# Moving seven of eight expert-output gathers and additions out of the expert layer and into the first tile of the cross attention

## The chip, the core and the metric

The kernel runs on one core of a Trainium2 chip. The metric is device time in microseconds (us) for one execution. A core has five engines that run their own instruction streams and meet through semaphores: PE (TensorE, matrix products, with its weight loads shown as PEld), DVE (VectorE), ACT (ScalarE), POOL (GpSimd) and SP (SyncE, which here issues the plain DMAs). POOL issues the indirect DMAs, which gather rows of memory by an index.

## The reference, cut to what matters

The model takes x, 16 x 64 tokens of width 512, and a context of 16 x 512 rows of width 384, and applies six layers, each as x = x + layer(layernorm(x)):

```
x = x + cosine similarity of x with the context
x = x + self attention (16 heads)
x = x + experts: 8 experts, each token goes to its best 2
x = x + cross attention to the context (16 heads of 64)
x = x + decayed attention, a scan
x = x + feed forward with rounding
```

The layer that the change starts in, in the reference:

```
scores = softmax(xf @ w_gate);  weights, idx = top_k(scores, 2)
...each expert computes its tokens' rows: exp_out...
gathered = exp_out[flat_e, pos_c]
w = weights.reshape(-1)[:, None] * vmask
out = (gathered * w).reshape(N, TOP_K, d).sum(axis=1)
```

So the last step of the expert layer is, for each token, to fetch two rows of 512 numbers and to add them to x, each times its weight. The layer behind it, the cross attention, begins with the layernorm of the new x:

```
q = x @ Wq;  k = context @ Wk;  v = context @ Wv
out = softmax(q k^T * scale) v @ Wo + bo
```

## The kernel before, in words

x stays in SBUF as [128 partitions, 8 token tiles (+1 spare), 512]; a token tile is 128 tokens. Everything is float32.

**Expert layer** (`expert_layer`, L636). A first block routes: the two best experts of each token, their weights (`top`), and the row (`slot`) that each copy of a token takes in a table in memory. A second block runs 23 steps; each loads 128 rows of the table and an expert's weights, multiplies (L901, L885) and stores 128 rows of results in `yg_d`, called routed_y in the profile. Behind the steps comes the part that the change touches. POOL (L971 to L980) waits for all stores, and then issues for each of the 8 token tiles two indirect gathers, one for each chosen expert, into `yb`, a buffer with room for 4 tiles. It is the old `xn`, called xnall in the profile. DVE (L960 to L968) waits for a tile's two gathers and does two `scalar_tensor_tensor` operations on it, x = gathered * weight + x (L963), the second after the first has ended. Nothing else runs on the core then.

Between layers the program clears the semaphores of the last layer on all engines (`reset_sems`, L2002) and opens those of the next (`open_sems`, L1992). All engines meet there, so the cross attention starts when DVE's last addition is done.

**Cross attention** (`cross_attention_layer`, L983). A start part computes for token tile 0 the layernorm (DVE statistics L131 to L134, one power on POOL L139, DVE L145, PE transposes L152), and the queries (L1120) and the queries through Wk (L1134). Then `tile(i)` runs for the 8 token tiles: seven in a loop, the last written out behind it. A tile has 16 pairs of heads g = 0 to 15 (PAIRS). For each pair, in a software pipeline over the engines:

- PE `scores` of pair g + 2 (split product of 9 matmuls, L106), then `turn` of pair g (4 transposes of the normalized exponentials, L1098), and at g = 5, 9 and 13 a `weigh` (36 matmuls, L106).
- ACT: `exponent` (L1203), then copies that take the high part of operands (L1207 to L1220).
- DVE, in this order in each g: the reciprocal (L1324), the normalization of `pb` (L1325, which `turn` waits for), `rest_q` for pair g + 3 (L1299, qs, which `scores` of that pair waits for), `rest_P` of pair g - 1 (L1299, pT), `maximum` of pair g + 2 (L1294), and in some g the low parts of the context, `rest_T` at g = 3 to 5 and `rest_N` at g = 0 to 3, 11 and 12 (L1299, cT and cN). At g = 6 and 7 come the next tile's layernorm statistics and L145.

Behind the 16 pairs PE does the next tile's queries, the last `weigh`, the head outputs (L1165), which ACT copies to the buffer `oT`, and the output product with `oT` (L1176), whose bias row `bo` (L1177) comes from W0. DVE adds the result to x (L1347). `oT` is thus written and read only near the end of a tile. POOL's only work in the layer is L139, once a tile.

The order on each engine is as written in the program; the position of an operation in DVE's stream is where the code of `tile` puts it.

Of the kernel before, what the change touches and what calls it, by code (L numbers as in the profile page):

```python
# [15 lines left out]
P = 128  # L16
# [54 lines left out]
BASE = 1  # L71
# [564 lines left out]
def expert_layer(nc, a, e):  # L636
# [13 lines left out]
    with ExitStack() as st:  # L650
# [3 lines left out]
        xn = sbuf("xnall3", [P, NT, D])  # L654
        slot = sbuf("slot3", [P, NT, 2], U32)
        top = sbuf("top3", [P, NT, 2])
        owner = sbuf("owner3", [1, ET], I32)
# [9 lines left out]
        y_mm, y_sb = sem("y_mm3"), sem("y_sb3")  # L667
        s_yb = [sem(f"s_yb3_{n}", pool_dma=True) for n in range(NT // 2)]
        added, half = sem("added3"), sem("half3")

# [154 lines left out]
        y = sbuf("y3", [P, 2, D])  # L825
        YB = NT // 2
        yb = xn
        TURNS = (ET - 3) // 2
# [11 lines left out]
        with nc.Block() as block:  # L840
# [97 lines left out]
            @block.vector  # L938
            def _(ve):
                def y_take(s, u, pair):  # L940
                    ve.wait_ge(y_mm, BASE + s + 1)
                    ve.wait_ge(y_out[u], BASE + 16 * pair)
                    nc.vector.tensor_copy(y[:, u, :], ps[7]).then_inc(y_sb, 1)

                def step(s, u, pair):
                    if not (isinstance(s, int) and s < 2):
                        y_take(s - 2, u, pair - 1)
                    ve.wait_ge(silu_sb, BASE + s + 1)
                    ve.wait_ge(gl_mm, BASE + s + 1)
                    ve.wait_ge(hT_mm, BASE + 2 * s)  # L950
                    for c in range(2):
                        ins = nc.vector.tensor_tensor(hid[:, c * HFE:(c + 1) * HFE], gated[:, c * HFE:(c + 1) * HFE],  # L952
                                                      ps[2 + c][:, 0:HFE], ALU.mult)
                    ins.then_inc(hid_sb, 1)

                steps(ve, step)
                y_take(ET - 2, 1, (ET - 2) // 2)
                y_take(ET - 1, 0, (ET - 1) // 2)

                for t in range(NT):  # L960
                    ve.wait_ge(s_yb[t % YB], 32 * (t // YB + 1))
                    for c in range(2):
                        ins = nc.vector.scalar_tensor_tensor(x[:, t, :], yb[:, t % YB * 2 + c, :], top[:, t, c:c + 1],  # L963
                                                             x[:, t, :], ALU.mult, ALU.add)
                        if c == 0:
                            ins.then_inc(half, 1)
                            ve.wait_ge(half, BASE + t + 1)
                    ins.then_inc(added, 1)  # L968

            @block.gpsimd  # L970
            def _(pool):  # L971
                for u in range(2):
                    pool.wait_ge(y_out[u], BASE + 16 * ((ET + 1 - u) // 2))
                for t in range(NT):
                    if t >= YB:
                        pool.wait_ge(added, BASE + t - YB + 1)
                    for c in range(2):
                        nc.gpsimd.indirect_dma_start(
                            out=yb[:, t % YB * 2 + c, :], out_offset=None, in_=yg_d,
                            in_offset=bass.IndirectOffsetOnAxis(slot[:, t, c:c + 1], axis=0)).then_inc(s_yb[t % YB], 16)  # L980


def cross_attention_layer(nc, a, e):  # L983
# [23 lines left out]
    with ExitStack() as st:  # L1007
# [14 lines left out]
        xT = W0[:, 15360:15872].rearrange("p (k t) -> p k t", k=DK)  # L1022
        bo = W0[0:1, 15872:16384]
        nmax, rsum, rinv = sbuf("nmax4", [P, 4]), sbuf("rsum4", [P, 4]), sbuf("rinv4", [P, 4])
# [6 lines left out]
        ct_hi, ct_lo, cn_hi, cn_lo = sem("ct_hi4"), sem("ct_lo4"), sem("cn_hi4"), sem("cn_lo4")  # L1031
        y_mm, added = sem("y_mm4"), sem("added4")
        work = [ps[4], ps[5], ps[7]]

# [8 lines left out]
        with nc.Block() as block:  # L1043
# [22 lines left out]
            @block.gpsimd  # L1066
            def _(pool):
                ln.pool(pool, 0)
                with pool.Fori(0, NT - 1) as i:
                    ln.pool(pool, i + 1)  # L1070

# [119 lines left out]
            def _(act):  # L1191
# [55 lines left out]
                def tile(i, last):  # L1247
# [19 lines left out]
                    if not last:  # L1267
                        queries(use + U_Q, U_Q)
                        for c in range(CK):
                            first_T(i + 1, 0, c)  # L1270
                    weighed(i, 3)
                    for n in range(2):
                        take(use + U_O + n, U_O + n, oT[:, 4 * n:4 * n + 4, :].rearrange("p m t -> p (m t)"))
# [15 lines left out]
            def _(ve):  # L1289
# [27 lines left out]

                def tile(i, last):
                    maximum(i, 0)
                    maximum(i, 1)  # L1320
                    for g in range(PAIRS):
# [12 lines left out]
                        for u, j in SPLIT_N.get(g, []):  # L1334
                            rest_N(i, u, j)
                        if g == 6 and not last:
                            ln.vector_stats(ch, i + 1)
# [16 lines left out]
                for g in range(QB):  # L1354
                    rest_q(0, g)
                with ve.Fori(0, NT - 1) as i:
                    ch.turn(i, 2 + PAIRS)
                    tile(i, False)
                ch.again(NT - 1)
                tile(NT - 1, True)  # L1360

# [583 lines left out]
def perceiver_kernel(nc, a, out):  # L1945

    ctx = ExitStack()
    with ctx:
# [67 lines left out]

        env = Env()
        env.x, env.cn, env.W0, env.PS, env.ps, env.ident, env.ones = x, cn, W0, PS, ps, ident, ones
        env.out, env.xg_d, env.yg_d, env.v_d, env.ba_d = out, xg_d, yg_d, v_d, ba_d
# [68 lines left out]
```

## Time and profile before

| | |
|---|---|
| time, median of 3 runs | 2352.98 us (2350.37 to 2353.34) |
| profiled execution: its own time | 2354.67 us |
| profiled execution: span of the trace | 2352.8 us |
| PE busy | 2090.8 us (89%) |
| DVE busy | 1084.6 us (46%) |
| ACT busy | 930.5 us (40%) |
| POOL busy | 123.4 us (5%) |

The span is cut into stretches by the layers: the expert layer's steps end at about 811 us, its gathers and additions at 839 us, and the cross attention runs from 844 to 1709 us in eight tiles of about 107 us. Busy shares are averages over all of it: in the 36 us from 810 to 846 us PE is busy for 0.48 us, in most of a cross attention tile for all of the time.

A row of a timeline reads: start in us, duration in us, engine, line, operation, output<-input, shape, count merged into this row, and in brackets how long the engine had been idle and what it waited for. PEld rows are PE's weight loads. "[... <-issue]" is a gap for which the profile shows no wait. Each of DVE's operations on 512 columns lasts longer than the step to the next one, since the next starts while it ends.

### The profile page before, as it was taken

The numbers are of one execution on the slowest core, as the hardware profiler recorded it, in microseconds if no ns is written. First come the engines' busy times: TensorE is split into PE (matmuls) and PEld (weight loads), VectorE is DVE, ScalarE is ACT, GpSimd is POOL, SyncE is SP. The second block draws the span as 40 slices with busy tenths as digits, with TensorE's granted clock in tenths as the row PEclk, the third lists the DMA queues.
The fourth block names the chain that finished last, engine by engine and source line by source line (L and its number), as shares of the span: only waits on it lengthen the run. The fifth ranks groups of instructions, "written<-read, shape, count | busy, mean of one in ns | idle before, by whom it ended". The sixth has DMA issues, their size and how long they took to land. (4 is left out here: it accounts for less than half of the span.)

```text
span 2352.8 us, 30151 instructions
## 1 busy us (share of the span) xinstructions
PE 2090.8 (89%) x9904; PEld 1469.2 (62%) x9904; DVE 1084.6 (46%) x2172; ACT 930.5 (40%) x1699; POOL 123.4 (5%) x138
## 2 busy tenths in 40 slices
PE   7979962999999759999999999999979499877999
PEld 5647862555555348787878777787757377633443
DVE  4655552010100135444352626343355599839992
ACT  5743320111111034445454545444344477615550
POOL 0000013000000110000000000000000000002220
PEclk9989875999999979999999999999989555588999
DMA  7410024777778421010000001010021700000000
GB/s 258 132 38 1 0 103 174 306 290 311 310 289 319 173 85 41 15 52 27 27 27 27 27 27 40 13 40 27 1 90 45 252 1 1 1 5 0 1 14 23
DMA packets 35591, 212.41 MB, mean 90 GB/s; under 512 B 5059, under 2 KB 5060, under 8 KB 27974
## 3 DMA queue, kind: packets, MB, share of 16 engines
q1 hardware_dynamic: 32966, 203.28, 22.9%
q0 software_dynamic: 2560, 8.39, 1.1%
q8 instruction: 25, 0.41, 0.1%
q14 instruction: 40, 0.33, 0.0%
HBM read 189.04 MB, written 22.61 MB: 90 GB/s over the span
## 5 line engine op out<-in xcount | busy, mean ns | idle before, releaser
L106 PE MATMUL PS<-cT,qs 128*128 128x512 f32 x1152 | 293.5, 400 | 7.0 <-ACT pb L1203 7.0
L106 PE MATMUL PS<-pT,cN 128*128 128x512 f32 x1152 | 270.3, 392 | 1.7 <-DVE pT L1299 1.7
L106 PEld LDWEIGHTS PS<-cT,qs 128*128 128x128 f32 x1152 | 208.4, 188 | 57.1 <-issue 15.1
L901 PE MATMUL PS<-W,xgT 128*128 128x384 f32 x736 | 242.8, 488 | 1.4 <-ACT xgT L924 1.4
L106 PEld LDWEIGHTS PS<-pT,cN 128*128 128x128 f32 x1152 | 213.9, 188 | 45.5 <-DVE pT L1299 1.9
L901 PEld LDWEIGHTS PS<-W,xgT 128*128 128x128 f32 x736 | 140.4, 191 | 104.2 <-issue 11.3
L1198 ACT ACTIVATE qp<-PS 128x512 f32<-128x512 f32 x192 | 110.9, 596 | 196.8 <-PE PS L106 189.8
L106 PE MATMUL PS<-ws,xT 128*128 128x512 f32 x672 | 170.2, 412 | 11.4 <-DVE ws L1510 6.3
L1294 DVE TENSOR_REDUCE nmax<-PS 128x1 f32<-128x512 f32 x128 | 87.7, 685 | 160.5 <-PE PS L106 160.4
L106 PEld LDWEIGHTS PS<-ws,xT 128*128 128x128 f32 x672 | 131.9, 200 | 46.8 <-issue 18.0
L952 DVE TENSOR_TENSOR hid<-gated,PS 128x384 f32<-128x384 f32 x46 | 23.4, 551 | 277.5 <-PE PS L877 235.6
L1705 PEld LDWEIGHTS PS<-cn,W1s 128*128 128x128 f32 x512 | 114.0, 328 | 49.5 <-DVE W1s L1633 45.3
L885 PE MATMUL PS<-W,hT 128*128 128x512 f32 x276 | 124.5, 600 | 10.4 <-ACT hT L918 10.4
L1705 PE MATMUL PS<-cn,W1s 128*128 128x16 f32 x512 | 120.8, 376 | 11.8 <-DVE W1s L1633 11.8
L1804 PE MATMUL PS<-xT,W 128*128 128x512 f32 x256 | 121.0, 624 | 6.4 <-ACT h L1847 5.6
L152 PE MATMUL PS<-cn,xn 128*128 128x128 f32 x200 | 40.7, 339 | 95.7 <-DVE xn L145 83.5
L1299 DVE TENSOR_TENSOR qs<-qp,qs 128x384 fp32r<-128x384 f32 x128 | 69.3, 552 | 115.4 <-ACT qs L1207 115.4
L1814 PE MATMUL PS<-W,hs 128*128 128x512 f32 x256 | 112.7, 592 | 0.5 <-DVE hs L1910 0.5
L1299 DVE TENSOR_TENSOR pT<-PS,pT 128x512 fp32r<-128x512 f32 x128 | 87.0, 685 | 56.1 <-ACT pT L1220 56.1
L931 ACT ACTIVATE gated<-PS 128x384 f32<-128x384 f32 x46 | 20.0, 488 | 227.2 <-PE PS L901 227.2
L139 POOL TENSOR_TENSOR rs<-ve,cn 128x1 f32<-128x1 f32 x51 | 28.0, 549 | 1561.9 <-DVE ve L134 1561.9
L1203 ACT ACTIVATE pb<-PS,nmax 128x512 f32<-128x512 f32 x128 | 87.5, 684 | 34.3 <-DVE nmax L1294 34.2
(225 smaller groups left out, 3161.1 us busy)
## 6 DMA issues: line engine op xcount, KB each, us to landing
W<-in_fc SPq DMA_DIRECT2D x23, 3072.0 KB, 12.6
W<-in_proj SPq DMA_DIRECT2D x23, 1536.0 KB, 6.7
cT<-in_ctxT SPq DMA_DIRECT2D x16, 768.0 KB, 5.7
ct_in<-in_ctxT SPq DMA_DIRECT2D x16, 768.0 KB, 4.3
cn_in<-in_ctxN SPq DMA_DIRECT2D x16, 768.0 KB, 5.0
W<-in_w SPq DMA_DIRECT2D x2, 4096.0 KB, 24.5
routed_x<-zero SPq DMA_DIRECT2D x23, 256.0 KB, 5.4
xg<-routed_x SPq DMA_DIRECT2D x23, 256.0 KB, 5.8
```

Of the source, the lines that this page charges most:

```text
L106: mm = nc.tensor.matmul(out, lhs(m, s), rhs(n, s), start=(opens and (s, m, n) == terms[0]), stop=((s, m, n) == terms[-1]))
L139: self.nc.gpsimd.tensor_tensor(self.rs[:, :], self.ve[:, :], self.cn[:, CN_MHALF:CN_MHALF + 1], ALU.pow).then_inc(self.rstd, 1)
L152: last = self.nc.tensor.transpose(self.bank[:, k * P:(k + 1) * P], self.xn[:, k * P:(k + 1) * P], self.ident)
L885: mm = nc.tensor.matmul(ps[7], hT[:, f, :], pj[u][:, f, :], start=(f == 0), stop=(f == FK - 1))
L901: mm = nc.tensor.matmul(ps[c][:, 0:HFE], xgT[:, k, :], fc[u][:, k, c * HFE:(c + 1) * HFE], start=(k == 0), stop=(k == DK - 1))
L1198: nc.scalar.activation(out, src, ACT.Copy, scale=scale).then_inc(w_sb, count)
L1203: nc.scalar.activation(pb[:, g % 2, :], ps[g % 2], ACT.Exp, bias=nmax[:, g % 4:g % 4 + 1], accum_out=rsum[:, g % 4:g % 4 + 1]).then_inc(e_ ...
L1294: nc.vector.tensor_reduce(nmax[:, g % 4:g % 4 + 1], ps[g % 2], AX.X, ALU.max, negate=True).then_inc(m_dve, 1)
L1299: return nc.vector.tensor_tensor(out, whole, first.bitcast(F32), ALU.subtract)
L1705: mm = nc.tensor.matmul(ps[u][:, col:col + B], rb[:, j % RB, k * P:(k + 1) * P], sel, start=True, stop=True)
L1804: mm = nc.tensor.matmul(ps[n % HB], w16[:, k, f * P:(f + 1) * P], xT[g][:, k, :], start=(k == 0), stop=(k == DK - 1))
L1814: mm = nc.tensor.matmul(ps[HB + t % ZB], hs[:, t // TG, f, (t % TG) * P:(t % TG + 1) * P], w26[:, f, :], start=(f == 0), stop=(f == FT - 1))
```

## The change

All but the first token tile's gathers and additions leave the expert layer. The expert layer gathers tile 0's two rows and adds them. In the cross attention POOL gathers tiles 1 to 7 one after the other into `oT` (seen as `got`, room for one tile), each gather waiting until the additions of the tile before have read the buffer (`routed`). DVE does tile t's two additions at the end of its work for pair g in tile 0: tile 1 at g = 1, then 2 at 3, 3 at 5, 4 at 8, 5 at 10, 6 at 12 and 7 at 14. POOL issues gathers 1 to 4, then does the power for tile 1's layernorm, then issues gathers 5 to 7. ACT waits for all additions ahead of its copies into `oT`.

So that this fits, `slot` and `top` move into a free place of W0, `bo` moves from W0 to the spare row of x, and DVE's tile 0 is written out ahead of its loop, which now runs over tiles 1 to 6. The loops of PE and ACT stay.

```diff
@@ expert_layer @@
-        slot = sbuf("slot3", [P, NT, 2], U32)
-        top = sbuf("top3", [P, NT, 2])
+        slot, top = e.slot, e.top
...
-                for t in range(NT):
-                    ve.wait_ge(s_yb[t % YB], 32 * (t // YB + 1))
-                    for c in range(2):
-                        ins = nc.vector.scalar_tensor_tensor(x[:, t, :], yb[:, t % YB * 2 + c, :], top[:, t, c:c + 1],
-                                                             x[:, t, :], ALU.mult, ALU.add)
-                        if c == 0:
-                            ins.then_inc(half, 1)
-                            ve.wait_ge(half, BASE + t + 1)
-                    ins.then_inc(added, 1)
+                ve.wait_ge(s_yb, 32)
+                for c in range(2):
+                    nc.vector.scalar_tensor_tensor(x[:, 0, :], xn[:, c, :], top[:, 0, c:c + 1], x[:, 0, :],
+                                                   ALU.mult, ALU.add).then_inc(half, 1)
+                    ve.wait_ge(half, BASE + c + 1)
...
-                for t in range(NT):
-                    if t >= YB:
-                        pool.wait_ge(added, BASE + t - YB + 1)
-                    for c in range(2):
-                        nc.gpsimd.indirect_dma_start(
-                            out=yb[:, t % YB * 2 + c, :], out_offset=None, in_=yg_d,
-                            in_offset=bass.IndirectOffsetOnAxis(slot[:, t, c:c + 1], axis=0)).then_inc(s_yb[t % YB], 16)
+                for c in range(2):
+                    nc.gpsimd.indirect_dma_start(
+                        out=xn[:, c, :], out_offset=None, in_=yg_d,
+                        in_offset=bass.IndirectOffsetOnAxis(slot[:, 0, c:c + 1], axis=0)).then_inc(s_yb, 16)
+                pool.wait_ge(s_yb, 32)
@@ cross_attention_layer @@
-        bo = W0[0:1, 15872:16384]
+        bo = x[0:1, NT, :]
...
+        got = oT[:, :, :].rearrange("p (c k) t -> p c (k t)", c=2)
+        ROUTED_AT = {1: 1, 3: 2, 5: 3, 8: 4, 10: 5, 12: 6, 14: 7}
@@ gpsimd @@
+                def gather(t):
+                    if t > 1:
+                        pool.wait_ge(routed, BASE + 2 * (t - 1))
+                    for c in range(2):
+                        nc.gpsimd.indirect_dma_start(
+                            out=got[:, c, :], out_offset=None, in_=e.yg_d,
+                            in_offset=bass.IndirectOffsetOnAxis(e.slot[:, t, c:c + 1], axis=0)).then_inc(s_got, 16)
                 ln.pool(pool, 0)
-                with pool.Fori(0, NT - 1) as i:
-                    ln.pool(pool, i + 1)
+                for t in range(1, 5):
+                    gather(t)
+                ln.pool(pool, 1)
+                for t in range(5, NT):
+                    gather(t)
+                pool.wait_ge(s_got, 32 * (NT - 1))
+                with pool.Fori(0, NT - 2) as i:
+                    ln.pool(pool, i + 2)
@@ scalar @@
+                    act.wait_ge(routed, BASE + 2 * (NT - 1))
                     for n in range(2):
                         take(use + U_O + n, U_O + n, oT[:, 4 * n:4 * n + 4, :].rearrange("p m t -> p (m t)"))
@@ vector @@
+                def add_routed(t):
+                    ve.wait_ge(s_got, 32 * t)
+                    for c in range(2):
+                        nc.vector.scalar_tensor_tensor(x[:, t, :], got[:, c, :], e.top[:, t, c:c + 1], x[:, t, :],
+                                                       ALU.mult, ALU.add).then_inc(routed, 1)
+                        ve.wait_ge(routed, BASE + 2 * (t - 1) + c + 1)
...
                         for u, j in SPLIT_N.get(g, []):
                             rest_N(i, u, j)
+                        if first and g in ROUTED_AT:
+                            add_routed(ROUTED_AT[g])
...
-                with ve.Fori(0, NT - 1) as i:
-                    ch.turn(i, 2 + PAIRS)
-                    tile(i, False)
+                ch.turn(0, 2 + PAIRS)
+                tile(0, True, False)
+                with ve.Fori(0, NT - 2) as i:
+                    ch.again(i + 1)
+                    tile(i + 1, False, False)
                 ch.again(NT - 1)
-                tile(NT - 1, True)
+                tile(NT - 1, False, True)
@@ perceiver_kernel @@
+        env.slot = W0[:, 15872:15888].bitcast(U32).rearrange("p (t c) -> p t c", t=NT)
+        env.top = W0[:, 15888:15904].rearrange("p (t c) -> p t c", t=NT)
```

## Rows read from the trace of the kernel before

**Rows 1.** The timeline of the expert layer's end, all engines.

```profile
818.35 1.54 DVE L963 SCALAR_TENSOR_TENSOR x<-xnall,top,x 128x512 f32<-128x512 f32 x2 [7.14 <-DMA xnall<-routed_y,slot]
818.55 1.37 POOL L978 DMA_INDIRECT xnall<-routed_y,slot  x1 [0.30 <-issue]
...
837.92 1.54 DVE L963 SCALAR_TENSOR_TENSOR x<-xnall,top,x 128x512 f32<-128x512 f32 x2 [1.40 <-DMA xnall<-routed_y,slot]
```

**Rows 2.** The gathers of L978 by their line: duration min/median/max, and landing.

```profile
L978 POOL DMA_INDIRECT xnall<-routed_y,slot x16: 942/952/1379, 813.5 to 834.2; - x16
...
DMA to landing us min/median/max: 3.4/3.7/3.9
```

**Rows 3.** The additions of L963 by their line: duration of one, min/median/max in ns.

```profile
L963 DVE SCALAR_TENSOR_TENSOR x<-xnall,top,x x16: 751/752/753, 818.3 to 838.7; 128x512 f32<-128x512 f32 x16
```

**Rows 4.** The timeline of the cross attention's start.

```profile
843.69 0.69 DVE L131 BATCH_NORM_STATS2 st<-x 128x6 f32<-128x512 f32 x1 [4.23 <-PEq L1994]
...
844.99 0.57 POOL L139 TENSOR_TENSOR rs<-ve,cn 128x1 f32<-128x1 f32 x1 [9.89 <-DVE ve L134]
...
846.20 1.12 PE L152 MATMUL PS<-cn,xn 128*128 128x128 f32 x4 [35.72 <-DVE xn L145]
```

**Rows 5.** Stretches: length, busy us (instructions) of each engine, PE clock, DMA share, GB/s.

```profile
409.00:410.00 1.00, 0.90 (x4) 0.71 (x4) 0.00 (x0) 0.00 (x0) 0.00 (x0) 0.50 0.88 356
413.00:414.00 1.00, 1.00 (x3) 0.63 (x2) 0.00 (x0) 0.00 (x0) 0.00 (x0) 0.57 1.32 555
...
814.00:816.00 2.00, 0.00 (x0) 0.00 (x0) 0.00 (x0) 0.00 (x0) 1.44 (x2) 0.50 0.35 82
...
854.00:855.00 1.00, 1.00 (x10) 1.00 (x10) 0.00 (x0) 0.10 (x1) 0.00 (x0) 0.91 0.00 0
...
938.00:955.00 17.00, 17.00 (x137) 15.28 (x137) 2.63 (x5) 4.55 (x8) 0.00 (x0) 1.00 0.15 47
```

**Rows 6.** The timeline of tile 0, pairs g = 2 to 7.

```profile
879.71 0.16 DVE L1324 RECIPROCAL rinv<-rsum 128x1 f32<-128x1 f32 x1
...
885.77 0.15 DVE L1324 RECIPROCAL rinv<-rsum 128x1 f32<-128x1 f32 x1
...
889.36 0.42 PEld L1098 LDWEIGHTS PS<-cn,pb 128*128 128x128 f32 x4 [0.48 <-DVE pb L1325]
...
889.78 8.44 PE L106 MATMUL PS<-pT,cN 128*128 128x512 f32 x36
...
891.49 0.16 DVE L1324 RECIPROCAL rinv<-rsum 128x1 f32<-128x1 f32 x1
...
900.29 0.69 DVE L1294 TENSOR_REDUCE nmax<-PS 128x1 f32<-128x512 f32 x1 [7.05 <-PE PS L106]
```

**Rows 7.** The timeline of tile 0, pairs g = 9 to 15.

```profile
907.18 0.49 DVE L1325 TENSOR_SCALAR pb<-pb,rinv 128x512 f32<-128x512 f32 x1
...
907.88 0.59 PEld L1098 LDWEIGHTS PS<-cn,pb 128*128 128x128 f32 x4
...
920.22 0.49 DVE L1325 TENSOR_SCALAR pb<-pb,rinv 128x512 f32<-128x512 f32 x1
...
920.62 0.55 DVE L1299 TENSOR_TENSOR qs<-qp,qs 128x384 fp32r<-128x384 f32 x1
...
921.95 0.69 DVE L1294 TENSOR_REDUCE nmax<-PS 128x1 f32<-128x512 f32 x1 [0.17 <-PE PS L106]
922.08 1.93 PEld L106 LDWEIGHTS PS<-cT,qs 128*128 128x128 f32 x9
...
926.68 0.16 DVE L1324 RECIPROCAL rinv<-rsum 128x1 f32<-128x1 f32 x1
...
927.42 0.42 PEld L1098 LDWEIGHTS PS<-cn,pb 128*128 128x128 f32 x4 [0.81 <-DVE pb L1325]
...
930.50 0.16 DVE L1324 RECIPROCAL rinv<-rsum 128x1 f32<-128x1 f32 x1
...
935.90 1.03 PEld L1098 LDWEIGHTS PS<-cn,pb 128*128 128x128 f32 x8
```

More of the change, by code:

```diff
@@ L667, in expert_layer @@
         y_mm, y_sb = sem("y_mm3"), sem("y_sb3")
-        s_yb = [sem(f"s_yb3_{n}", pool_dma=True) for n in range(NT // 2)]
-        added, half = sem("added3"), sem("half3")
+        s_yb = sem("s_yb3", pool_dma=True)
+        half = sem("half3")
         def load_fc(sp, u, own):
@@ L825, in expert_layer @@
         y = sbuf("y3", [P, 2, D])
-        YB = NT // 2
-        yb = xn
         TURNS = (ET - 3) // 2
@@ L1032, in cross_attention_layer @@
         y_mm, added = sem("y_mm4"), sem("added4")
+        s_got, routed = sem("s_got4", pool_dma=True), sem("routed4")
+        got = oT[:, :, :].rearrange("p (c k) t -> p c (k t)", c=2)
+        ROUTED_AT = {1: 1, 3: 2, 5: 3, 8: 4, 10: 5, 12: 6, 14: 7}
         work = [ps[4], ps[5], ps[7]]
@@ L1316, in rest_P, with tile @@
                          turned(pT[0], g)).then_inc(pt_sb, 1)
-                def tile(i, last):
+                def add_routed(t):
[4 more added lines that the diff above has]
+                        ve.wait_ge(routed, BASE + 2 * (t - 1) + c + 1)
+                def tile(i, first, last):
                     maximum(i, 0)
```

## The prediction, made before the changed kernel was run

> **What bounds the kernel now.** I read the timeline across the layer boundary first, then the two operations of the moved part by their lines, then tile 0 of the cross attention pair by pair, asking at each place for an addition who waits for DVE there.
>
> At the expert layer's end nothing runs but the gathers and the additions. DVE begins tile 0's two additions at 818.35 and tile 7's at 837.92, each pair 1.54 us long, and idles for gathers between them [rows 1]. The next layer's first statistics start at 843.69, 4.23 us after the last addition, and DVE waited there for the meeting of the engines [rows 4]. So the seven tiles' share of the tail stands on the path whole.
>
> Tile 0 of the cross attention has two kinds of stretches. Between the `weigh` blocks DVE works without a gap from g = 1 to g = 5 and PE waits for it: the reader is to see the 0.48 us in front of `turn(5)` at 889.36, put down to DVE's `pb`, and the 0.81 us before `turn(13)` at 927.42 [rows 6, 7]. During a `weigh`, 36 matmuls in 8.44 us from 889.78 on, it is DVE that idles: 7.05 us until 900.29 [rows 6]. An addition in the first kind costs its length; in the second it is free. Behind the last pairs PE is busy without a gap (17.00 of 17.00 us from 938 to 955, [rows 5]), and DVE's next tile start hangs on PE, so a shift that PE has by `weigh(2)` is carried to the end and is not given back.
>
> **What it removes.** The meeting of the engines follows tile 0's additions instead of tile 7's: 837.92 - 818.35 = 19.57 us off the path [rows 1]. The 4.23 us between the layers stay [rows 4]; a few semaphores fewer to clear I count as nothing. Tile 0's own gathers come as before, so nothing new is late there.
>
> **What the additions cost in tile 0.** One lasts 752 ns with hardly any spread [rows 3]; two with the wait between them take 1.54 us [rows 1], and the wait behind the second, which before had only the layer's end behind it, adds another 0.04. So 1.58 us per token tile, in order of the stream:
>
> - Tiles 1 and 2, at g = 1 and 3: in the stretch where DVE has no gap. Everything behind them to `pb` of pair 5 shifts, and `turn(5)`, which already waited, shifts with it. 2 x 1.58 = 3.16 us.
> - Tile 3, at g = 5: behind `pb` of pair 5. PE is in `weigh(0)`; DVE has 7.05 us [rows 6]. 0.
> - Tile 4, at g = 8: before `pb` of pair 9, ready at 907.18 + 0.49 = 907.67 where `turn(9)` loads at 907.88 [rows 7]: slack 0.2. 1.4 us.
> - Tile 5, at g = 10. The code puts it behind `maximum` of pair 12, whose scores come only behind `weigh(1)`; so it isn't hidden by that block, but stands before the normalization at 920.22. `rest_q` at 920.62 feeds the scores at 922.08, and the `maximum` at 921.95 had waited only 0.17 [rows 7]. 1.58 - 0.17 = 1.4 us.
> - Tile 6, at g = 12, before the reciprocal at 926.68; `turn(13)` waits for DVE already [rows 7]. 1.58 us.
> - Tile 7, at g = 14, before the reciprocal at 930.50, while PE is in `weigh(2)` until 935.90 [rows 7]. The normalization of pair 15 would end at 931.2, so there is room for 4.7 us. 0.
>
> Sum 3.16 + 1.4 + 1.4 + 1.58 = 7.54 us.
>
> **Whether the gathers come in time.** One buffer now serves all, so gather t + 1 is asked for when additions t have ended. From there to data: 0.1 for POOL to see it (my choice, from the power that starts right behind the statistics, [rows 4]), 0.95 for the first issue, 0.30 to the next [rows 1, 2], 3.7 from the second's issue to its landing [rows 2]. 5.05 us. DVE's own work between two additions is the time it has: 885.77 - 879.71 = 6.06 us for tile 2; 891.49 - 885.77 = 5.72 for tile 3, and 5.5 more of idle [rows 6]; over 13 for tiles 4 and 5; 926.68 - 920.22 + 0.2 = 6.66 for tile 6; 930.50 - 926.68 = 3.82 for tile 7, which waits 1.2 and with its additions uses 2.8 of the 4.7 that are free [rows 7]. All fit, tile 2 by 1.0 us. Tile 1's is asked for at the layer's start and is early by far. Behind POOL's waits stands only the power for tile 1's layernorm, behind gather 4, which is issued some 5 us before DVE's statistics at g = 6; 0. No plain DMA is queued behind the gathers, as SP issues those. They share the DMA engines with the context loads, which could hold gather 7 up; it has 1.9 us left.
>
> Two prices no row shows. POOL now issues gathers while DVE is busy with other operations than the additions. A gather that met additions took 1.37 instead of 0.95 us and ended with them, at 819.92, while no addition was slowed (751 to 753 ns) [rows 1 to 3]. By that only the gathers lengthen, by 0.4 each at most or 5.9 us in all, still under 6.06. At worst normalizations behind additions 1, 2, 4 and 5 wait out an issue of 0.95, or both: up to 7.6 us. At best 0. I take 0.8, near the rows, which show the additions untouched.
> The Trainium skill, in "SBUF — State Buffer", section "Who interferes with whom", says that DVE in a two-port mode and GpSimd exclude each other for a whole instruction, whoever came first. The row above agrees on the side of the gather; for DVE's side no row here has a normalization beside a gather. By that rule the upper end would be the case, and it is the first rival below.
>
> The PE clock: PE is at 0.50, that is 1.2 GHz, by 814, and will be so when the layer begins in either kernel. It is at full clock 7.9 us after PE's first work at 846.20 here, but 4.8 us after that at 409.1 at the expert layer's start [rows 4, 5]. So it may come up to 3.1 us sooner, worth half of that: -1.6 to, by symmetry, +1.6. I take -0.5.
>
> The wait on ACT ahead of `oT` is long met when it comes. DVE's written-out tile, the moved `bo`, `slot` and `top` do the same operations: 0, with nothing beside them that could hide a price.
>
> **The sum.** -19.57 + 7.54 + 0.8 - 0.5 = -11.7 us. The profiled execution, 2354.67 us around a span of 2352.8, would become 2343.0. It lies 1.69 above the median of the runs shown, 2352.98, from which I forecast 2341.3 us.
>
> **The rivals.**
> - DVE and POOL exclude each other. For it: the lengthened gather. Against it: the untouched additions. Price: four normalizations wait 0.95 or twice that, 3.8 to 7.6 in place of 0.8: 2344.3 to 2348.1.
> - The additions find more room than I see: part of the shift is made up when PE comes out of a `weigh` with DVE's work done, and the clock rises early. For it: `turn` waits under a microsecond for DVE. Against: the waits are of the right engine, and nothing idles on PE that could absorb. 2 us less on the additions and 1.1 on the clock: 2338.2.
> - The gathers become the bound. If DVE starves POOL until one request takes G instead of 5.05 us, additions 2, 3, 6 and 7 wait G - 6.06, G - 11.2, G - 6.66 and G - 6.95 (3.82 and the 3.1 of room left). It decides from G = 10.5 on, where the first, third and fourth sum to 11.8, the whole gain. At G = 12: 5.9 + 0.8 + 5.3 + 5.1 = 17.1, so 2358.4. Against it: the longest of 16 issues was 1.38 us, with two-input additions beside it.
> - It does not do what it says, and the end of the layer was held by something beside the seven tiles (the meeting itself, or POOL's waits): no difference, 2353. Against: DVE's rows wait for gathers one by one.
>
> **How the numbers follow.** Forecast 0.60 (its own range 2339.5 to 2343.7, from the ends of clock and waits), exclusion 0.23, more room 0.09, gathers the bound 0.04, no difference 0.04. What this measurement can tell from no change is 0.2%, 4.7 us, so 2348.3 and below is faster: 0.60 + 0.23 + 0.09 less a little of the exclusion's upper end gives 0.91; same 0.05; slower 0.04. The range leaves out the last two and the very end of the first: 2337.5 to 2347.5.
>
> **What would show it.** The statistics that start the cross attention at about 824.1 instead of 843.69. Seven `scalar_tensor_tensor` pairs of 1.54 us in tile 0. `weigh(0)` 3.2 us later behind the layer's start than before, `weigh(1)` 4.6, `weigh(2)` 7.5. DVE waiting for a gather only before tile 7's, about 1.2 us. Wrong if DVE waits for gathers at g = 3 or 12, if normalizations (L1325) last over their 0.49 us, if POOL's issues last 2 us or more, or if tile 1 is shifted otherwise than `weigh(2)`.

## The result, and the profile after

The changed kernel takes 2341.13 us (median of 5 runs, 2338.00 to 2342.99) against 2352.98 us before (5 runs, 2348.99 to 2353.34). The medians differ by 11.9 us. The ratio, taken between the means, is 0.9954, 95% interval 0.9942 to 0.9967: 0.46% or 10.8 us faster. Predicted were 2341.3 us, 2337.5 to 2347.5. Run again beside the first experiments it took 2342.34 us against 2352.68, ratio 0.9954 (0.9940 to 0.9968).

The profiled execution of the changed kernel took 2338.00 us around a span of 2336.1, 16.7 us less than that of before, more than the medians differ by. Cut at landmarks, the two spans say why:

| stretch | before | after | difference |
|---|---|---|---|
| start to the expert layer's first gather | 813.50 | 809.97 | -3.53 |
| first gather to the cross attention's first statistics | 30.19 | 10.56 | -19.63 |
| those to the addition of tile 0's output into x | 131.59 | 140.31 | +8.72 |
| that to the addition of tile 7's output | 732.52 | 732.56 | +0.04 |
| that to the end | 645.0 | 642.7 | -2.3 |

The first and the last row lie in code that the change leaves alone; they are spread between executions. In the repeat the first gather comes at 811.32 and the last stretch is 644.7. The change itself is -19.63 + 8.72 = -10.9 us.

The tail of the expert layer after the change, in the timeline (start us, us, engine, line; in brackets the idle time before), answers to [rows 1] and [rows 4]:

```profile
809.97 0.98 POOL L968 DMA_INDIRECT xnall<-routed_y,W  x1 [411.64 <-SPq L837]
811.25 0.96 POOL L968 DMA_INDIRECT xnall<-routed_y,W  x1 [0.30 <-issue]
814.63 1.54 DVE L959 SCALAR_TENSOR_TENSOR x<-xnall,W,x 128x512 f32<-128x512 f32 x2 [6.95 <-DMA xnall<-routed_y,W]
820.53 0.69 DVE L131 BATCH_NORM_STATS2 st<-x 128x6 f32<-128x512 f32 x1 [4.35 <-PEq L2017]
```

One pair of additions where eight stood, and the same 4.35 us between the layers (4.23 before).

DVE's stream in tile 0 with the additions in it, from the same timeline:

```profile
856.41 1.53 DVE L1332 SCALAR_TENSOR_TENSOR x<-oT,W,x 128x512 f32<-128x512 f32 x2
857.98 0.16 DVE L1342 RECIPROCAL rinv<-rsum 128x1 f32<-128x1 f32 x1
...
864.05 1.53 DVE L1332 SCALAR_TENSOR_TENSOR x<-oT,W,x 128x512 f32<-128x512 f32 x2
...
871.36 1.53 DVE L1332 SCALAR_TENSOR_TENSOR x<-oT,W,x 128x512 f32<-128x512 f32 x2
...
880.18 0.69 DVE L1304 TENSOR_REDUCE nmax<-PS 128x1 f32<-128x512 f32 x1 [5.49 <-PE PS L106]
...
912.73 0.69 DVE L1343 TENSOR_SCALAR pb<-pb,rinv 128x512 f32<-128x512 f32 x1
...
915.72 1.54 DVE L1332 SCALAR_TENSOR_TENSOR x<-oT,W,x 128x512 f32<-128x512 f32 x2 [1.07 <-DMA oT<-routed_y,W]
917.30 0.16 DVE L1342 RECIPROCAL rinv<-rsum 128x1 f32<-128x1 f32 x1
```

From the start of an addition pair to the next reciprocal is 1.57 us. The pair at 871.36 is paid from idle time, which is 5.49 us now and was 7.05 [rows 6]; only tile 7's waits for its gather, 1.07 us. What PE sees, in its timeline (weight loads of the transposes, and the `weigh` blocks):

```profile
866.37 0.42 PEld L1107 LDWEIGHTS PS<-cn,pb 128*128 128x128 f32 x4 [2.53 <-DVE pb L1343]
...
869.64 8.45 PE L106 MATMUL PS<-pT,cN 128*128 128x512 f32 x36
...
890.04 8.46 PE L106 MATMUL PS<-pT,cN 128*128 128x512 f32 x36
...
911.48 0.42 PEld L1107 LDWEIGHTS PS<-cn,pb 128*128 128x128 f32 x4 [2.41 <-DVE pb L1343]
...
911.89 10.06 PE L106 MATMUL PS<-pT,cN 128*128 128x512 f32 x36
```

The last line is the one thing that nobody had in the sum: the same 36 matmuls take 10.06 us, not 8.46. The stretches show the cause (columns as in [rows 5], the clock third from the end):

```profile
905.00:908.00 3.00, 2.62 (x14) 1.87 (x13) 2.96 (x8) 1.89 (x5) 0.19 (x1) 1.00 0.52 156
912.00:913.00 1.00, 1.00 (x6) 0.81 (x5) 0.96 (x4) 0.34 (x1) 0.78 (x1) 0.79 0.99 336
913.00:914.00 1.00, 1.00 (x3) 0.73 (x3) 0.47 (x2) 0.92 (x3) 0.17 (x1) 0.50 0.63 205
915.00:916.00 1.00, 1.00 (x4) 0.81 (x3) 0.28 (x1) 0.00 (x0) 0.00 (x0) 0.51 0.10 37
916.00:917.00 1.00, 1.00 (x5) 0.80 (x5) 0.96 (x2) 0.49 (x1) 0.00 (x0) 1.00 0.00 0
```

PE's clock fell from 2.4 to 1.2 GHz at 912.6, just after PE had waited for DVE before turn(11), (12) and (13), and came back at 916. Its weight loads had idled 0.87, 0.81 and 2.41 us there; in the kernel before they idle only before turn(13), 0.81 us [rows 7].

### The profile page after: what moved, and what is told of

The parts are those of the page before. It is cut to its first block and busy times, and to the rows that moved or that the text cites. A ratio compares the mean times of both kernels' runs of the same rounds, so it can differ in the third digit from the quotient of the medians.

```text
span 2336.1 us, 30096 instructions
## 1 busy us (share of the span) xinstructions
PE 2090.7 (89%) x9904; PEld 1465.4 (63%) x9904; DVE 1084.3 (46%) x2172; ACT 930.7 (40%) x1699; POOL 121.7 (5%) x138
## 5 line engine op out<-in xcount | busy, mean ns | idle before, releaser
L106 PEld LDWEIGHTS PS<-ws,xT 128*128 128x128 f32 x672 | 131.8, 199 | 46.3 <-issue 17.8
```

Of the source, the lines that this page charges most:

```text
L106: mm = nc.tensor.matmul(out, lhs(m, s), rhs(n, s), start=(opens and (s, m, n) == terms[0]), stop=((s, m, n) == terms[-1]))
```

## The experiments

In all of them "tile 0" is the time from the cross attention's first statistics to the addition of tile 0's output, and "the rest" that from the addition of tile 7's output to the end. A `weigh` is given by its start behind the first statistics. Collected from their traces (us; the clock's rise is where PE came to full clock in the start part, to half a microsecond):

| run | tile 0 | weigh(0), (1), (2) | clock's rise | clock's dips in tile 0 | rest |
|---|---|---|---|---|---|
| before | 131.59 | 46.09, 65.20, 84.14 | 10.5 | none | 645.0 |
| changed | 140.31 | 49.11, 69.51, 91.36 | 10.0 | at 92 to 95.5 | 642.7 |
| repeat | 140.03 | 48.89, 69.27, 91.10 | 9.5 | at 91.5 to 95 | 644.7 |
| idle places | 130.23 | 44.67, 63.99, 82.91 | 7.5 | none | 645.1 |
| tile 6 later | 137.10 | 49.12, 69.53, 89.76 | 7.5 | at 45 to 48.5 | 645.2 |
| none | 130.95 | 45.58, 64.73, 83.67 | 9.5 | none | 634.1 |
| one gather | 138.68 | 49.16, 69.53, 91.34 | 7.5 | at 45 to 49 | 644.1 |
| late gathers | 144.69 | 51.96, 72.35, 96.23 | 10.0 | at 47.5 to 51 and at 95 to 98.5 | 643.8 |
| rearranged only | 130.69 | 45.28, 64.44, 83.35 | 9.0 | none | 644.4 |
| idle places, 43 more | 131.75 | 46.21, 65.53, 84.47 | 10.5 | none | 646.6 |
| idle places, 230 more | 130.51 | 44.99, 64.28, 83.17 | 7.5 | none | 636.0 |
| idle places, 212 more | 131.16 | 45.65, 64.96, 83.88 | 9.5 | none | 636.1 |
| before, 72 more | 131.62 | 46.10, 65.26, 84.20 | 10.5 | none | 637.9 |

**Does the dip repeat?** The changed kernel, unchanged.

> The changed kernel again, unchanged, to see what repeats. Measured from the cross attention's first statistics (L131) to the addition of tile 0's output into x, tile 0 took 131.6 us before and 140.3 after: 7.2 us of shift by turn(13), as predicted, and 1.6 us more in weigh(2) (10.06 us instead of 8.46), in which the PE clock was at half from 912.8 to 916. My theory: the additions leave PE waiting before turn(11) to turn(13), and the clock falls for it; then the dip comes again, in weigh(2) or near it, and tile 0 takes 139 to 141 us. Rival: a chance dip that has nothing to do with the change; then it is absent here and tile 0 takes 138.7 us. Time 2341 us; the 3.5 us that the profiled execution was ahead of the one before when the expert layer ended are chance by both and may be gone.

2342.34 us. The dip is there again, in the same block, which takes 10.04 us. It is no chance event of one execution. The expert layer's first gather is at 811.32 instead of 809.97.

**The additions where DVE idles.**

```diff
-        ROUTED_AT = {1: 1, 3: 2, 5: 3, 8: 4, 10: 5, 12: 6, 14: 7}
+        ROUTED_AT = {}
+        EARLY_AT = {6: 4, 10: 5, 14: 6}
...
+                        if first and g in EARLY_AT:
+                            add_routed(EARLY_AT[g])
                         if g + 2 < PAIRS:
                             maximum(i, g + 2)
...
                     rest_P(i, PAIRS - 1)
+                    if first:
+                        add_routed(7)
...
                 ln.vector_norm(ve, 0)
+                add_routed(1)
+                add_routed(2)
                 for c in range(CK):
                     rest_T(0, 0, c)
                 for g in range(QB):
                     rest_q(0, g)
+                add_routed(3)
```

> The same gathers and additions, only at places in DVE's stream where it idles: tiles 1 and 2 between the layernorm and the first rest_T (DVE idle 13.3 us there), tile 3 behind the three rest_q ahead of tile 0, tiles 4 and 5 at g = 6 and 10 ahead of the maximum that waits for a weigh, tile 6 in weigh(2) at g = 14, tile 7 behind the last rest_P. My theory (the additions cost their 1.58 us only where PE waits for DVE, and the clock dip follows from these waits): tile 0 takes 131.6 to 132.4 us instead of 140.3, no dip, time 2341.1 - 8.5 = 2332.6 us. Rival 1 (the gathers themselves, by POOL, the port shared with DVE or DMA traffic, are what costs): tile 0 stays near 138 to 140 us and the time at 2339 to 2341. Rival 2 (gather 2 misses its place, as the room for it is only 0.9 us): 1 to 3 us of the gain are lost, 2334 to 2335.

2333.30 us (2332.53 to 2334.24), ratio to before 0.9917 (0.9904 to 0.9931): 8 to 9 us better than the changed kernel, as expected. Tile 0 takes 130.23 us. Against before all three `weigh` blocks are 1.2 to 1.4 us early. The clock's earlier rise, 3 us at half speed, gives up to 1.6 of that, so at most 0.4 us of seven gathers and fourteen additions is left on the path. The cleaner comparison is between two runs of the table in which the clock rose at the same time: with the additions at idle places (the run with 212 more) tile 0 takes 131.16 us, without any ("none") 130.95. Their price is 0.2 us for all seven. In the timeline, the additions of tile 3 wait 2.88 us for their gather, where PE does not need DVE, and those of tile 4 stand ahead of the `maximum`:

```profile
846.85 1.54 DVE L1333 SCALAR_TENSOR_TENSOR x<-oT,W,x 128x512 f32<-128x512 f32 x2 [2.88 <-DMA oT<-routed_y,W]
...
871.07 1.53 DVE L1333 SCALAR_TENSOR_TENSOR x<-oT,W,x 128x512 f32<-128x512 f32 x2
```

**Only tile 6's additions later.**

```diff
-        ROUTED_AT = {1: 1, 3: 2, 5: 3, 8: 4, 10: 5, 12: 6, 14: 7}
+        ROUTED_AT = {1: 1, 3: 2, 5: 3, 8: 4, 10: 5, 13: 6}
...
                     rest_P(i, PAIRS - 1)
+                    if first:
+                        add_routed(7)
```

> Only the additions of tile 6 move, from g = 12 to g = 13 (into weigh(2)), and those of tile 7 behind the last rest_P of the tile. By the prediction's step for tile 6 turn(13) comes 1.58 us sooner. If the wait of 2.0 us before turn(13) was what let the clock fall, the dip goes too: tile 0 takes 140.3 - 1.6 - 1.6 = 137.1 us, time 2338 us. If the dip is chance, or comes from the waits at turn(11) and turn(12) as well, 138.7 us with it and 137.1 without, in no relation to the edit. If the step is wrong (PE would have waited there anyhow), 140.3.

2339.88 us (2334.29 to 2340.91), tile 0 at 137.10. Tile 0's time is the expected one, but not by the expected parts, and the whole kernel's is 1.9 us above the expected 2338. From weigh(1) to weigh(2) it takes 20.23 us against 21.85 in the changed kernel: 1.62, the step for tile 6. Against the 18.94 of before, 1.29 are left, which is tile 5's. The dip did not go. It moved, to 45 us, in front of weigh(0), where the additions of tiles 1 and 2 make PE wait. There it ate the 1.3 us that an early rise of the clock had given: the additions of tile 1 are 1.29 us earlier than in the changed kernel (34.59 against 35.88), weigh(0) is not (49.12 against 49.11). The stretch of the dip, columns as in [rows 5]:

```profile
869.00:872.50 3.50, 3.50 (x12) 2.78 (x11) 3.46 (x8) 2.20 (x5) 1.12 (x2) 0.53 0.52 149
```

So the wait before turn(13) is one place at which the clock can fall, not the only one.

**Neither gathers nor additions in tile 0.**

```diff
-        ROUTED_AT = {1: 1, 3: 2, 5: 3, 8: 4, 10: 5, 12: 6, 14: 7}
+        ROUTED_AT = {}
...
                 ln.pool(pool, 0)
-                for t in range(1, 5):
-                    gather(t)
                 ln.pool(pool, 1)
-                for t in range(5, NT):
-                    gather(t)
-                pool.wait_ge(s_got, 32 * (NT - 1))
...
-                    act.wait_ge(routed, BASE + 2 * (NT - 1))
```

> Leaves out the gathers and additions of tiles 1 to 7 altogether, so that x lacks the experts' share in these tiles. What is left of the change is the shorter expert tail, the moved buffers and DVE's written-out tile. My theory: tile 0 takes 131.5 us as before, the cross attention starts 10.6 us after the first gather as in the changed kernel, time 2341.1 - 8.8 = 2332.3 us. Rival (the written-out tile costs something, by its code or its first run): tile 0 is 1 us or more above 131.6.

2323.27 us, 9 us less than expected. Tile 0 and the tail are as expected, 130.95 and 10.80. The difference is in the rest, 634.1 us where the runs above had 642.7 to 645.2. The larger part of it, 7.5 us, is in a scan loop of the next layer that the edit does not touch: from DVE's first to its last operation there it takes 180.4 us instead of 187.9 in the two runs of the changed kernel. Nothing of the kind was expected; the last four runs are about it.

**One gather for all additions.**

```diff
-                for t in range(1, 5):
-                    gather(t)
+                gather(1)
                 ln.pool(pool, 1)
-                for t in range(5, NT):
-                    gather(t)
-                pool.wait_ge(s_got, 32 * (NT - 1))
+                pool.wait_ge(s_got, 32)
...
-                    ve.wait_ge(s_got, 32 * t)
+                    ve.wait_ge(s_got, 32)
```

> The additions stay where the changed kernel has them, but only tile 1 is gathered; the additions of tiles 2 to 7 add tile 1's rows again (with their own weights), so x is not the reference's there. It takes away six of the seven gathers from POOL, from the DMA engines and from DVE's waits. My theory: the gathers cost nothing where they stand, so tile 0 takes 140.2 us again, with the dip of the PE clock in weigh(2), time 2341 to 2342 us. Rival (DVE and POOL exclude each other, or the wait of 1.1 us before tile 7's additions reaches PE): tile 0 takes 1 us or more less than in the changed kernel.

2340.55 us against 2341.13 and 2342.34 with all gathers. Tile 0 is 1.4 to 1.6 us shorter, which by the number alone would speak for the rival. The blocks say otherwise: weigh(0) to weigh(1) takes 20.37 us and weigh(1) to weigh(2) 21.81, in the changed kernel 20.40 and 21.85. The difference is weigh(2) itself, 8.46 us, since the dip lay at 45 us here. Six gathers cost under 0.1 us. Whether a dip falls before weigh(0), where PE waits anyhow, or into weigh(2) moves the time by more than that, and goes with where in the start part the clock had risen (7.5 us in both runs with the early dip, 9.5 to 10 in those with the late one). The next run, with longer waits, has a rise at 10 and a dip at either place.

**Gathers 3 us late.**

```diff
                         pool.wait_ge(routed, BASE + 2 * (t - 1))
+                        for k in range(5):
+                            nc.gpsimd.tensor_tensor(W0[:, 15904 + 5 * t + k:15905 + 5 * t + k], cn[:, CN_HALF:CN_HALF + 1],
+                                                    cn[:, CN_MHALF:CN_MHALF + 1], ALU.pow)
```

> POOL does five small powers (0.55 us each) ahead of the gathers of tiles 2 to 7, so that a gather takes G = 8.0 us from its request to its data instead of the 5.0 measured. The prediction's rule for late gathers: additions 2, 3, 6 and 7 wait G - 6.06, G - 11.2, G - 6.66 and G - 6.95 beyond what is hidden, so 1.9 + 0 + 1.3 + 1.1 = 4.3 us: tile 0 takes 140.2 + 4.3 = 144.5 us, and more if the longer waits of PE bring further dips of the clock (1.6 us each), time 2345 to 2348 us. Rival: DVE's waits overlap those it had, or the additions of tiles 4 and 5 are late as well: tile 0 below 142 or above 148.

2345.49 us, ratio to before 0.9973 (0.9963 to 0.9983); tile 0 at 144.69. DVE's waits for gathers, in its timeline:

```profile
868.62 1.54 DVE L1335 SCALAR_TENSOR_TENSOR x<-oT,W,x 128x512 f32<-128x512 f32 x2 [1.66 <-DMA oT<-routed_y,W]
...
878.59 1.54 DVE L1335 SCALAR_TENSOR_TENSOR x<-oT,W,x 128x512 f32<-128x512 f32 x2 [2.00 <-DMA oT<-routed_y,W]
...
916.64 1.54 DVE L1335 SCALAR_TENSOR_TENSOR x<-oT,W,x 128x512 f32<-128x512 f32 x2 [1.58 <-DMA oT<-routed_y,W]
...
926.18 1.54 DVE L1335 SCALAR_TENSOR_TENSOR x<-oT,W,x 128x512 f32<-128x512 f32 x2 [4.03 <-DMA oT<-routed_y,W]
```

From the start of tile 1's additions to tile 2's it is 9.41 us, less 1.57 for the additions: G = 7.8. Tiles 2 and 6 wait 1.66 and 1.58 us, about what the rule said (1.9 and 1.3); tile 3's wait is hidden as it said, since weigh(0) to weigh(1) takes 20.39 us here and 20.40 in the changed kernel; tile 7's was to cost 1.1 and costs nothing, since weigh(2) to the tile's end takes 48.5 us here and 48.9 in the changed kernel. In its place there is a second dip of the clock, one from 47.5 to 51 and one from 95 to 98.5, of which 1.15 us fall into weigh(2) (9.61 us). Tile 0 is as long as expected, but one part of the sum is not what was expected.

**The rearrangement alone.** The kernel before with these edits:

```diff
-        slot = sbuf("slot3", [P, NT, 2], U32)
-        top = sbuf("top3", [P, NT, 2])
+        slot, top = e.slot, e.top
...
-        bo = W0[0:1, 15872:16384]
+        bo = x[0:1, NT, :]
...
-                with ve.Fori(0, NT - 1) as i:
-                    ch.turn(i, 2 + PAIRS)
-                    tile(i, False)
+                ch.turn(0, 2 + PAIRS)
+                tile(0, False)
+                with ve.Fori(0, NT - 2) as i:
+                    ch.again(i + 1)
+                    tile(i + 1, False)
...
+        env.slot = W0[:, 15872:15888].bitcast(U32).rearrange("p (t c) -> p t c", t=NT)
+        env.top = W0[:, 15888:15904].rearrange("p (t c) -> p t c", t=NT)
```

> The kernel before with nothing but the rearrangement of the change: slot and top in W0, bo in the spare row of x, DVE's tile 0 written out ahead of its loop. My theory: no price, tile 0 takes 131.6 us (131.0 to 131.8), time 2352.7 us. Rival: the longer program of DVE moves the later loops in the instruction stream. In the run without additions three stalls of 2.6 us on DVE in the scan of the next layer, which the profile puts down to issue, are gone, though that code is the same; if placement does this, they may be gone here too, and the time some 8 to 10 us less.

2352.41 us, ratio 1.0002 (0.9992 to 1.0011): no price. Tile 0 is 0.9 us shorter by an earlier rise of the clock, and the stalls in the scan are all there, 8.4 us in three.

**Where the scan's stalls come from.** Four runs. The first three start from the kernel with the additions at idle places. The first of them puts 43 increments of an unused semaphore (`pad`) into DVE's stream ahead of the last tile:

```diff
                 ch.again(NT - 1)
+                for _ in range(43):
+                    ve.sem_inc(pad)
                 tile(NT - 1, False, True)
```

> The kernel with the additions at DVE's idle places, and 43 increments of an unused semaphore in DVE's stream ahead of the last cross attention tile, where DVE idles. In the run without gathers and additions the rest of the kernel behind the last cross attention tile took 634.1 us instead of 645, with three issue stalls of 2.6 us fewer in DVE's scan loop. Its DVE program is about 21 instructions shorter; 43 more is the same place by a raster of 64, 32 or 16 instructions. Theory A (the place of the loop in the instruction stream decides): the rest takes 634 to 636 us, time 2323 to 2325. Theory B (the data: x without the experts' share in seven tiles): the stalls stay, 645 us, time 2333.5. If A holds with another raster than these, the stalls stay too, so only the first outcome decides.

2338.85 us: slower than without the 43 by 5.5 us between the medians and 5.2 between the profiled executions. Of the 5.2, 1.5 are in tile 0 by a late rise of the clock, 1.8 between it and tile 7's output, where the 43 stand, and 1.5 in the rest. The scan itself is 4.1 us longer, 192.0 us against 187.9; the part before it happens to be 2.3 us shorter. The stalls did not go; there are more. DVE's waits in the scan, by their sum, times and longest, for this kernel:

```profile
DVE W1s L1650 <- issue: 7.6, 3, 2.6
DVE W1s L1655 <- issue: 3.6, 3, 1.2
```

and for the kernel before:

```profile
DVE W1s L1617 <- issue: 7.8, 3, 2.7
```

The data are the same in this run as in the one without the 43, and so is the scan's code. So the place of the code changes the stalls, though not in the raster that was expected. The next two put 230 and 212 where DVE idles in the last tile:

```diff
                     rest_P(i, PAIRS - 1)
                     if first:
                         add_routed(7)
+                    if last:
+                        for _ in range(230):
+                            ve.sem_inc(pad)
```

> The kernel with the additions at DVE's idle places, and 230 increments of an unused semaphore in DVE's stream, this time in the last cross attention tile behind the last rest_P, where DVE idles for over 20 us. The Trainium skill, in 'Runtime: NRT & Kernel Launch', section 'Instruction fetch mechanics', says that an engine holds two blocks of 256 instructions and that a branch to a block outside them waits for a fetch. By that, the scan's loop stalls at each of its three jumps back unless it starts early enough in a block; the run without additions (some 14 to 22 instructions fewer, no stall, 26 instruction packets on queue q14 instead of 40) would just fit, the others just not, and a move by 256 less these 14 to 22 would bring it to fit again; 230 is meant to overshoot by a few. Theory A (place in the instruction stream): no issue stall in the scan, about 26 packets on q14, the rest behind the last cross attention tile 634 to 636 us instead of 645.1, time 2323 to 2325 us. Theory B (the stalls went for another reason, such as the data of the run without additions): three stalls of 2.6 us or more stay, 645 us or more, time 2333.

> As the run with 230 increments, with 212. By theory A the loop lies 18 instructions earlier in its block: still without stalls if it starts at least so far into a block, otherwise it begins in the block before and stalls return. Either outcome bounds the room; the rest behind the last cross attention tile is 634 to 636 us, or 643 and more.

2325.41 us with 230 (2324.50 to 2326.88), ratio to before 0.9885 (0.9868 to 0.9901), and 2325.33 in the one execution with 212. The rest is 636.0 and 636.1 us, 9 less than without them, and the scan itself 180.3 and 180.2 instead of 187.9. DVE's scan has one wait left, the first. For the kernel with 230, its waits there and its DMA queues:

```profile
DVE W1s L1651 <- ACT W1s L1693: 13.3, 1, 13.3
```

```profile
q8 instruction: 25, 0.41, 0.1%
q14 instruction: 27, 0.22, 0.0%
```

For the kernel before:

```profile
q14 instruction: 40, 0.33, 0.0%
```

The packets that fetch instructions went from 40 to 27 with the stalls. Of the versions that do all of the work this is the fastest: 27 us or 1.15% less than before, and 16 less than the changed kernel in its own runs. The last run puts 72 into the kernel before, at the same place:

```diff
                     rest_P(i, PAIRS - 1)
+                    if last:
+                        for _ in range(72):
+                            ve.sem_inc(pad)
```

> The kernel before, with nothing but 72 increments of an unused semaphore in DVE's stream in the last cross attention tile, behind the last rest_P. DVE's program ahead of the scan is some 100 to 107 instructions shorter there than in the kernel that lost its stalls with 212 and with 230; blocks of 256 then put the loop at the same place with 56 to 81. If the place of the scan's loop in the instruction stream is all there is to it, the three issue stalls go here as well, tile 0 stays at 130.2 to 131.7 us, and the time is 2352.5 - 9 to 10 = 2343 us, without any of the change. Rival (the gain needs the changed kernel, or my count of instructions is off by more than the room): the stalls stay and the time is 2352.

2343.91 us, ratio to before 0.9962 (0.9948 to 0.9976): 26 packets on q14, no stall, the scan 180.4 us instead of 188.7, the rest 637.9. 72 instructions that do nothing give 0.38%, nearly as much as the 0.46% of the change under study. And the two add up: between this kernel and the one with 230, both without stalls, the medians differ by 18.5 us, near the 19.6 that the tail is worth.

## Why the prediction was right

The sum held: -11.7 forecast, -11.9 between the medians, -10.8 between the means, -10.9 by the landmarks within the two profiled executions. The large terms were right for the reasons given. That the small ones came out 0.8 us off and not more is partly luck: two prices were too high by 0.7 and 0.2 us, and the clock's was too low by 1.9. The hit on the median, within 0.2 us, is luck too. Two of the prediction's own signs of being wrong came up: one normalization lasted longer than 0.49 us, in both profiled executions of the changed kernel, and tile 1 is shifted by 8.7 us where weigh(2) is by 7.2. The second is the step that failed, the last below. Point by point, by its steps:

- **The tail.** -19.57 forecast, -19.63 measured. It was read off DVE's own rows, and nothing else held the end of the layer: the time between the layers is 4.35 us where it was 4.23 [rows 4]. The rival that it does not do what it says is out.
- **The additions, 7.54 us.** Shifts against before were to be 3.2 at weigh(0), 4.6 at weigh(1) and 7.5 at weigh(2); measured are 3.0, 4.3 and 7.2, each with 0.2 off that belongs to the clock's slightly earlier rise. Behind the start of weigh(2) tile 0 is, but for the dip, 0.1 us shorter than before, so the term measures 7.3. Free places cost next to nothing: the run at idle places shows 0.2 us for all seven at once. The run that moved tile 6's additions shows 1.62 for a step of 1.58, and 1.3 for tile 5's of 1.4. Tile 5's is the one that reads against intuition: in the code it stands behind an operation that waits for a `weigh`, and is therefore not covered by that block. Put ahead of that operation, as in the run at idle places, it is part of the 0.2 us for all seven.
- **The gathers in time.** G was 5.05; from the start of tile 6's additions less 1.57 to tile 7's it is 5.0. Tile 7's wait was 1.07 us for 1.2. The 3.7 us to landing did not hold for all: tile 4's two gathers took 5.9 and 6.0, which its long room hid. With gathers at G = 7.8 the rule was about right for tiles 2, 3 and 6 and too dear for tile 7.
- **DVE against POOL, 0.8 us.** Too much. POOL's fourteen issues took 946 to 991 ns (in other runs single ones up to 1.31 us), and of the normalizations beside them one took 0.69 us instead of 0.49 (at 912.73) and the others at most 0.02 more; with six gathers away the two stretches between the `weigh` blocks change by less than 0.1. The rival of exclusion falls. The Trainium skill, in "SBUF — State Buffer", section "Who interferes with whom", says that one engine blocks the other for the whole instruction while DVE is in a two-port mode. No run shows in which mode DVE worked here. The one row of 0.69 us agrees with the rule at most in part, and as a price it would have been four to eight times 0.95 us.
- **The clock, -0.5 us.** The step that failed, in size and in sign: the rise gave -0.2, and the prediction looked at the start part only. Behind the waits that the additions put on PE the clock fell later in the tile, 1.6 us in weigh(2). Of the sum's two small terms, 0.8 and -0.5, measured are about 0.1 and 1.6 - 0.2 = +1.4: the clock is off by 1.9 us, and the ports made up 0.7 of it.

That the dip follows from the additions is shown by its presence in all five runs that have them at places where PE waits (changed, repeat, tile 6 later, one gather, late gathers) and its absence in all eight that do not, one profiled execution each. Which of PE's waits it takes is not shown. Why it falls at 45 us in two, at 92 in two and at both places in the run with late gathers is not settled: in the first four it goes with the rise of the clock in the start part, the fifth has the late rise and both dips, and no run forces the rise.

## What to carry to other kernels

To hide work behind another engine's block, put it in front of the operation that waits for that block, not behind it: behind it is the first place that is not covered. On a core where PE is the bound, price an addition on DVE, where PE waits for it, at its length plus what a fallen PE clock costs (here 1.3 to 1.6 us a dip). And when two versions differ by some microseconds in code that neither touched, look for issue stalls at loops before explaining them by the edit.

## What the runs showed that was not expected

**Where a loop lies in the instruction stream is worth 8 to 9 us here.** DVE's scan loop of the decayed attention stalls for 2.5 to 2.9 us at each of its three jumps back in the kernel before and in most versions. 212 or 230 idle instructions ahead of it, 72 in the kernel before, or the 14 additions and their waits left out, take the stalls away, and 43 add three of 1.2 us, 2 us behind each jump. The scan takes 187.9 to 188.7 us with three stalls, 192.0 with six and 180.2 to 180.4 with none; the other microseconds by which the rests differ lie outside it and vary between runs. The instruction packets on one queue fall from 40 or 41 to 26 to 28 with the stalls. The Trainium skill, in "Runtime: NRT & Kernel Launch", section "Instruction fetch mechanics", says that an engine holds two blocks of 256 instructions and that a branch to a place outside them waits for a fetch; the count of 72 to add to the kernel before was worked out with its figure, and the run agrees. The figure itself is not singled out: by the instruction counts in the expectations, blocks of 128 would fit the runs too. The same section calls the cost of running on across the end of a block mostly hidden and gives no time for the wait at a branch; the three measured here come to 7.8 us of 2353. That the change's own longer DVE program left the stalls as they were (645.0 and 642.7 to 644.7 us of rest) is luck: it could have gained or lost this much by itself.

**The clock in the start part rises anywhere from 7.5 to 10.5 us behind the layer's first statistics**, in programs that are nearly alike up to there. At 1.2 instead of 2.4 GHz half of the 3 us is lost, and 1.5 us is also the spread of tile 0 among the runs that have no dip (130.2 to 131.8 us).
